# Output slices beside the next image's scan: TensorE adds the two directions in the PSUM bank, VectorE gates from PSUM, ScalarE's copies stand ahead of its decays

## What is computed

```python
xn = layernorm(x) * ln_g + ln_b                       # over the 96 channels
x, z = (xn @ W_in)[..., :192], (xn @ W_in)[..., 192:]
x = silu(causal_conv(x, conv_w, conv_b))              # 4 taps
proj = x @ W_xproj
dt = softplus(proj[..., :6] @ W_dt + b_dt)
h_t = exp(dt_t * A) * h_(t-1) + dt_t * B_t * x_t      # 192 channels x 16 states
y_t = sum over states of h_t * C_t, + x_t * D
out = (y * silu(z)) @ W_out                           # 192 -> 96
```

## Time and profile before

| | |
|---|---|
| time, median of 3 runs (lowest, highest) | 6072.25 us (6064.57, 6073.67) |
| the profiled execution: its own time | 6072.92 us |
| its span in the trace | 6071.1 us |
| VectorE busy, share of the span | 5288.1 us, 87% |
| GpSimd busy | 5088.1 us, 84% |
| TensorE busy (matmuls) | 4711.1 us, 78% |
| ScalarE busy | 3204.5 us, 53% |

### The profile page before, as it was taken

How to read it: one execution, slowest core, us unless ns; L and a number is a source line. 1 busy time by engine, 2 the same in 40 slices (tenths; PEclk the granted TensorE clock), 3 DMA queues, 4 the chain that set the end, 5 groups by cost and what they waited for, 6 DMA issues and landing times. The chain is left out here.

```text
span 6071.1 us, 73617 instructions
## 1 busy us (share of the span) xinstructions
PE 4711.1 (78%) x17230; PEld 1200.4 (20%) x17230; DVE 5288.1 (87%) x3523; ACT 3204.5 (53%) x5159; POOL 5088.1 (84%) x2405
## 2 busy tenths in 40 slices
PE   7998757777777777777777777777777777777788
PEld 6775211111111111111111111111111111111122
DVE  3223749999999999999999999999999999999943
ACT  1224645555555555555555555555555555555533
POOL 0000349999999999999999999999999999999965
PEclk9999876666676666666666666666666666666689
DMA  1002755555555555555555555555555555555599
GB/s 35 28 28 67 213 152 183 184 183 183 184 184 184 184 184 182 182 181 181 182 181 181 182 183 184 184 184 183 182 182 184 184 184 182 183 183 182 182 260 274
DMA packets 351020, 1048.25 MB, mean 173 GB/s; under 512 B 66820, under 2 KB 101430, under 8 KB 300556
## 3 DMA queue, kind: packets, MB, share of 16 engines
q1 hardware_dynamic: 336652, 1022.72, 53.2%
q10 hardware_dynamic: 14336, 25.17, 1.3%
HBM read 836.01 MB, written 211.63 MB: 173 GB/s over the span
## 5 line engine op out<-in xcount | busy, mean ns | idle before, releaser
L1259 POOL TENSOR_TENSOR hc<-hring,c_rep 128x1024 f32<-128x1024 f32 x1541 | 3597.5, 2361 | 18.9 <-DVE hring L1222 13.6
L1222 DVE TENSOR_TENSOR_SCAN hring<-decay,carry,u_ps 128x1024 f32<-128x1024 f32 x1221 | 2827.7, 2333 | 44.3 <-POOL hc L1259 44.3
L1029 PE MATMUL u_ps<-stack_b,w_spread 48*128 48x512 bf16 x2442 | 1053.8, 523 | 908.0 <-DVE hring L1222 904.0
L1116 ACT ACTIVATE decay<-dt_rep,w_a 128x1024 f32<-128x1024 f32 x1222 | 1399.5, 1147 | 675.2 <-DVE hring L1222 662.4
L1204 DVE TENSOR_TENSOR u_ps<-u_ps,u_rep 128x1024 f32<-128x1024 f32 x1221 | 1471.5, 1205 | 68.3 <-DMA u_rep<-u_scr 56.4
L1047 PE MATMUL y_ps<-hc,w_gather 128*32 128x512 f32 x6144 | 1212.4, 874 | 0.0
L1116 ACT ACTIVATE u_ps<-dt_rep,w_a 128x1024 f32<-128x1024 f32 x322 | 360.0, 1118 | 1360.7 <-DVE hring L1222 1360.7
L1246 POOL TENSOR_TENSOR drive_p<-u_rep,b_rep 128x1024 f32<-128x1024 f32 x322 | 760.2, 2361 | 11.1 <-DMA u_rep<-u_scr 11.1
L1222 DVE TENSOR_TENSOR_SCAN hring<-u_ps,carry,drive_p 128x1024 f32<-128x1024 f32 x321 | 751.3, 2341 | 11.6 <-ACT decay L1116 11.6
L666 POOL TENSOR_TENSOR xs<-xc_ln,rs 96x512 f32<-96x512 f32 x64 | 90.3, 1411 | 701.9 <-ACT rs L650 684.2
L1029 PEld LDWEIGHTS u_ps<-stack_b,w_spread 48*128 48x128 bf16 x2442 | 147.4, 101 | 2407.3 <-DVE hring L1222 2004.4
(11 more groups left out here) (108 smaller groups left out, 3966.9 us busy)
## 6 DMA issues: line engine op xcount, KB each, us to landing
dt_rep<-dt_scr SPq DMA_DIRECT2D x194, 1024.0 KB, 5.8
u_rep<-u_scr SPq DMA_DIRECT2D x194, 1024.0 KB, 7.7
c_rep<-bc_scr SPq DMA_DIRECT2D x260, 512.0 KB, 4.0
b_rep<-bc_scr SPq DMA_DIRECT2D x130, 512.0 KB, 4.2
xn<-xn_scr SPq DMA_DIRECT2D x132, 384.0 KB, 5.4
y_scr<-y_sb SPq DMA_DIRECT2D x768, 64.0 KB, 1.6
xn<-xn_scr SPq DMA_DIRECT2D x132, 256.0 KB, 4.7
dt_scr<-dt_sb SPq DMA_DIRECT2D x260, 128.0 KB, 2.1
```

The lines of the kernel that those rows point to most:

```text
L1029: mm = nc.tensor.matmul(u_ps[nv % NSLOT][:, sl], w["spread"][:, q, :], upper(stack_b[drv][:, sl]), start=True, stop=True)
L1116: nc.scalar.activation(to[:, :], dt_rep[r][:, b, :], ACT.Exp, scale=w["a"][:, col:col + 1]).then_inc(decay_ready, 1)
L1222: nc.vector.tensor_tensor_scan(hring[nv % NHR][:, ::step], factor[:, ::step], term[:, ::step], carry[:, drv, nv:nv + 1], ALU.mult, ALU.add ...
L1259: nc.gpsimd.tensor_tensor(hc[nv % NHC][:, :], hring[nv % NHR][:, :], c_rep[q][:, :], ALU.mult).then_inc(c_applied, 1)
```

## The change

In the scan, phases 8 to 63 each also finish one slice of 512 tokens of the image before. `run` has two new tasks. "gate" stands in the phase ahead of a slice: SP loads the slice in step 15 (seven DMAs), TensorE makes z in steps 20 and 22 into `prep_ps`, and ScalarE copies it to `z_sb` a step later each time. "slice" stands in the phase of the slice itself: in steps 0 and 10 TensorE adds the two directions by matmuls with the identity, both into the bank (512 columns, then 256), and VectorE multiplies the bank by `z_sb` into `y_bwd`; Silu of z (768 columns) is done beside that of x in step 0; in step 12 TensorE projects, in step 13 ScalarE copies to `res`, in step 14 SP stores to `out`. Channels stand here as 128 partitions x 512 and, for the last 64 channels, two halves of the tokens on 64 partitions each x 256. The output stage handles only the last image's 8 slices, with the same code in straight line (`over_last`) on buffers of its own. The loop over `it` is cut in three: iterations 0 to 2, 3 written out, 4 to 31. The three j of a conv group now stand together, in steps 14, 16 and 18. ScalarE does in each step what copies out of `prep_ps` first, and its decay last. The weights `z`, `out` and `ident` are prepared in `pointwise`.

```diff
@@ weights, pointwise @@
+            loads.append((self.out_w[rows, col, :], d["w_out"][lo:hi, h, :]))
+        loads.append((w["z"][:, :], d["w_in"][:, DI:2 * DI]))
+        loads.append((w["ident"][:, :], d["ident"]))
...
+                nc.vector.memset(w["out"][:, 1:3, :], 0.0)
...
+                nc.vector.tensor_copy(w["out"][:, 0, :], mixer.out_w[:, 0, :])
+                for s in range(2):
+                    nc.vector.tensor_copy(w["out"][64 * s:64 * s + 64, 1 + s, :], mixer.out_w[64 * s:64 * s + 64, 1, :])
@@ scan: steps @@
-        CONV_AT = ((10, 11, 12), (14, 15, 16), (18, 19, 20))
+        CONV_AT = ((14, 14, 14), (16, 16, 16), (18, 18, 18))
...
+        SLICE_AT, Z_AT = 15, (20, 22)
+        SUM_Y_AT, PROJECT_AT, RES_AT, OUT_STORE_AT = (0, 10), 12, 13, 14
+        CHANNELS = (slice(0, SL), slice(SL, SL + SL // 2))
+        SLICE_DMAS = 7
+        OUT_LAG = 2 * CHUNKS
@@ scan: SP @@
+                def gate(m, k, it, dr):
+                    if m == SLICE_AT:
...
+                        wait(sp, z_made, made, k)
+                        wait(sp, y_sum, summed_y, k)
+                        wait(sp, projected, free, k)
+                        sp.wait_ge(y_stored, stored)
+                        sp.dma_start(xz[:, :], d["xn_scr"][image, :, bass.ds(at + HALO, SL)]).then_inc(slice_in, 16)
+                        for to, scr in ((y_fwd, d["y_scr"][0]), (y_bwd, d["y_scr"][1])):
+                            sp.dma_start(to[:, 0:SL], scr[image, 0:P, bass.ds(at, SL)]).then_inc(slice_in, 16)
+                            for s in range(2):
+                                sp.dma_start(to[64 * s:64 * s + 64, SL:], scr[image, P:DI, bass.ds(at + s * (SL // 2), SL // 2)]).then_inc(slice_in, 16)
@@ scan: TensorE @@
+                            if g == 0 and slicing:
+                                pe.wait_ge(res_ready, pn - 1 - OUT_LAG)
...
+                        if slicing:
+                            pe.wait_ge(gated, 2 * (pn - 1 - OUT_LAG) + 1)
...
+                def gate(m, k, it, dr):
+                    if m == Z_AT[0]:
+                        pe.wait_ge(slice_in, 16 * SLICE_DMAS * (k + 1))
+                        pe.wait_ge(prep_out, NPREP * (k + OUT_LAG + 1) + 3)
+                        nc.tensor.matmul(prep_ps[:, :], w["z"][:, 0:P], xz[:, :], start=True, stop=True).then_inc(z_made, 1)
...
+                def slice_out(m, k, it, dr):
+                    for h in range(2):
+                        if m == SUM_Y_AT[h]:
...
+                            to = prep_ps[:, 0:SL // (h + 1)]
+                            nc.tensor.matmul(to, w["ident"][:, :], y_fwd[:, CHANNELS[h]], start=True, stop=False)
+                            nc.tensor.matmul(to, w["ident"][:, :], y_bwd[:, CHANNELS[h]], start=False, stop=True).then_inc(y_sum, 1)
+                    if m == PROJECT_AT:
+                        pe.wait_ge(gated, 2 * k + 2)
...
-                run(pe, ("front", front), ("back", back), ("prep", prep), ("conv", conv))
+                run(pe, ("front", front), ("back", back), ("prep", prep), ("slice", slice_out), ("conv", conv), ("gate", gate))
@@ scan: ScalarE @@
+                        if slicing:
+                            act.wait_ge(z_out, 2 * (pn - OUT_LAG))
+                            nc.scalar.activation(z_sb[:, :], z_sb[:, :], ACT.Silu).then_inc(z_silu, 1)
...
+                        nc.scalar.copy(z_sb[:, 0:SL], prep_ps[:, :]).then_inc(z_out, 1)
...
+                        nc.scalar.copy(res[:, :], prep_ps[0:C, :]).then_inc(res_ready, 1)
...
-                run(act, ("back", back), ("front", front), ("prep", prep), ("conv", conv))
+                run(act, ("back", back), ("prep", prep), ("slice", slice_out), ("conv", conv), ("gate", gate), ("front", front))
@@ scan: VectorE @@
+                def slice_out(m, k, it, dr):
+                    for h in range(2):
+                        if m == SUM_Y_AT[h]:
+                            dve.wait_ge(y_sum, 2 * k + h + 1)
+                            if h == 0:
+                                dve.wait_ge(z_silu, k + 1)
+                            nc.vector.tensor_tensor(y_bwd[:, CHANNELS[h]], prep_ps[:, 0:SL // (h + 1)], z_sb[:, CHANNELS[h]], ALU.mult).then_inc(gated, 1)
-                run(dve, ("front", front))
+                run(dve, ("front", front), ("slice", slice_out))
@@ output @@
-                over_slices(pe, (2, make_z), (0, project))
+                over_last(pe, (2, make_z), (0, project))
```

More of the change, by code:

```diff
@@ L88, in over_slices, with over_last @@
     image(B - 1, last=True)
+def over_last(eng, *stages):
+    most = max(lead for lead, _ in stages)
+    for s in range(-most, NS):
+        for lead, what in stages:
+            if 0 <= s + lead < NS:
+                what(s + lead)
 def after(eng, sem, count):
@@ L716, in scan @@
         b3 = sb("b3", [P, 3, P])
+        y_fwd = sb("y_fwd", [P, SL + SL // 2])
+        y_bwd = sb("y_bwd", [P, SL + SL // 2])
+        z_sb = sb("z_sb", [P, SL + SL // 2])
+        xz = sb("xz", [C, SL])
+        res = sb("res", [C, SL])
         u_ps = [ctx.enter_context(nc.psum_tensor(f"u_ps{i}", [P, 2 * SL], F32)) for i in range(NSLOT)]
@@ L828, in ahead @@
                         if has == kind:
-                            what(m, pn, 0, pn)
+                            what(m, pn, 0, pn, False)
             ahead("conv", 0)
@@ L837, in run, with iteration @@
             ahead("conv", 1)
-            with eng.Fori(0, ITERS) as it:
+            def iteration(it, gates, slices):
                 for dr in range(2):
@@ L849, in run @@
                             elif kind == "prep":
-                                what(m, p + 1, it + dr, 1 - dr)
-                            else:
-                                what(m, p + 2, it + 1, dr)
+                                what(m, p + 1, it + dr, 1 - dr, slices[dr])
+                            elif kind == "conv":
+                                what(m, p + 2, it + 1, dr, slices[dr])
+                            elif kind == "gate" and gates[dr]:
+                                what(m, p + 1 - OUT_LAG, it + dr, 1 - dr)
+                            elif kind == "slice" and slices[dr]:
+                                what(m, p - OUT_LAG, it, dr)
                     for kind, what in tasks:
@@ L991, in back @@
                                              y_sb[at:at + 32, :]).then_inc(y_stored, 16)
-                run(sp, ("front", front), ("prep", prep), ("conv", conv), ("back", back))
+                def gate(m, k, it, dr):
+                    if m == SLICE_AT:
+                        image, at = slice_of(it)
+                        at = at + dr * SL
+                        made, summed_y, free, stored = ready(2 * k, 2 * k, k, 64 * NG * (k + OUT_LAG - 1))
+                        wait(sp, z_made, made, k)
[8 more added lines that the diff above has]
+                def slice_out(m, k, it, dr):
+                    if m == OUT_STORE_AT:
+                        image, at = slice_of(it)
+                        made, = ready(k + 1)
+                        sp.wait_ge(res_ready, made)
+                        sp.dma_start(d["out"][image, :, bass.ds(at + dr * SL, SL)], res[:, :]).then_inc(out_stored, 16)
+                run(sp, ("front", front), ("prep", prep), ("conv", conv), ("back", back), ("gate", gate), ("slice", slice_out))
                 LAST = 2 * ITERS
                 sp.wait_ge(y_stored, 16 * 4 * NG * LAST)
+                sp.wait_ge(slice_in, 16 * SLICE_DMAS * (LAST - OUT_LAG + 1))
+                sp.wait_ge(out_stored, 16 * (LAST - OUT_LAG))
                 sp.wait_ge(xn_in, 96 * (LAST + 2))
@@ L1382, in _, with multiply @@
-                over_slices(act, (3, gate), (0, store))
+                    act.wait_ge(res_ready, s + 1)
+                    act.dma_start(d["out"][B - 1, :, s * SL:(s + 1) * SL], res[:, r, :]).then_inc(o_stored[r], 16)
+                over_last(act, (3, gate), (0, store))
             @block.vector
             def _(dve):
-                def multiply(b, s):
+                def multiply(s):
                     r = s % R
-                    dve.wait_ge(y_sum, NS * b + s + 1)
-                    dve.wait_ge(z_silu, NS * b + s + 1)
-                    after(dve, projected, NS * b + s - R + 1)
+                    dve.wait_ge(y_sum, s + 1)
+                    dve.wait_ge(z_silu, s + 1)
+                    after(dve, projected, s - R + 1)
```

121 lines of the change are left out of this document (82 added, 39 removed).

## The result

The changed kernel takes 5833.51 us (median of 4 runs, 5826.85 to 5833.89) beside 6071.51 for the kernel before on the same chip: ratio 0.9607, 95% interval 0.9591 to 0.9624, so 238 us faster. The forecast was 5864 us, with 5838 as the lower end. Direction, mechanism and the great term held; the time lies 30 us under the point and 4 us under the range.

What follows compares the result with a forecast made beforehand. GpSimd, late by its one wait a phase for ScalarE's `soft`, was taken to hold VectorE in the scan. 6072.9 - 225 (output stage) - 7 + 3 (VectorE) + 1 (before the scan) + 19 (TensorE) = 5864 us; range 5838 to 5945.

Steps and rivals of the forecast that it cites:

- What bound the scan: Scan: GpSimd's wait for `soft`, 1.14 us a phase, holds VectorE twice, 0.87 us a phase; ScalarE's new order removes it.
- Output stage: Stage after the scan: 8 of 64 slices stay, so it takes about 46.4 us and 225 us go.
- Gates: Scan, 56 phases: two VectorE multiplications, PSUM by SBUF, 0.60 and 0.33 us, together 0.93 us a phase.
- First failed step: VectorE in the scan: unheld it needs 75.52 us a phase, 76.45 with gates; +3 us in 56 phases, -7 in eight.
- Second failed step: TensorE in the scan: one late triple of conv j, 1.3 us, in four phases; +19 us, bounds nothing and 250.
- the sum by it, 5845: Forecast without TensorE's term, on the skill's account that more matmuls make each matmul faster: 5845 us.
- DMA hidden: Scan: slice loads and store, about 1.2 MB a slice, cost nothing, with only 2 to 5 us of cover.
- Before the scan: Pointwise stage: one memset and three small copies, some 0.7 us, entered as +1 us.
- 2: Rival, scan: TensorE late in many phases, costing VectorE 1 to 3.5 us each; 5909 to 6069 us; chance 0.18.
- 4: Rival, scan: TensorE becomes the bound, kernel slower than before; up to 634 us lost, or 6479 us; chance 0.04.
- 3: Rival, scan: GpSimd's wait remains or slice loads land late, gates' 0.93 us on top; 5916 to 5940 us; chance 0.09.
- 5: Rival, more gain: output stage under 40 us and no loss on TensorE; below 5838 us; chance 0.03.

Runs made afterwards that it cites:

- experiment 1: Kernel before, only ScalarE's order changed: copies out of `prep_ps` first in each step, decay last; 5994.58 us, ratio 0.9877.
- experiment 2: Kernel after with ScalarE's old order, decays ahead of what copies out of the bank; 5885.77 us, ratio 0.9696.
- experiment 6: Kernel after, but ScalarE copies each sum from the bank to `y_fwd` and VectorE's gates read SBUF only; 6127.82 us (one run).
- experiment 4: Kernel after with the last j of each conv group one step later; 5826.69 us, ratio 0.9602.
- experiment 3: Kernel before, only the three j of each conv group together, in steps 14, 16 and 18; 6070.1 us (one run).
- experiment 8: Kernel after with the slice loads issued four steps later, step 19 instead of 15; 6177.03 us (one run).

## Why the prediction was right, and where it was wrong

- **What bound the scan** (GpSimd's one wait for `soft` holds VectorE twice; ScalarE's decay to a PSUM slot holds `soft`): shown by experiments 1 and 2, which take the wait away and bring it back alone.
- **Output stage**, 46.4 forecast, 44.4 measured. In the profile it starts at 5787.47, its first z at 5794.93, and the last copy is at 5828.37.
- **Gates**, 0.93 a phase forecast, 76.15 - 75.23 = 0.92 measured. The price held because one operand is in PSUM, as in the row it was taken from; experiment 6 shows what another operand would have made of it.
- **First failed step: "VectorE, if nothing held it, 76.39 - 0.87 = 75.52".** It is 75.23 (experiments 1 and 4, where it waits for nothing). I took off the listed waits, but each of the two costs some 0.08 us more, and a delay of 0.06 that no row lists comes on top; what is left of the 0.29 was not found. So the 56 phases were to be 0.06 longer and are 0.24 shorter: 0.30 x 56 = 17 us, with 1.4 more in the others. That is over half of the miss.
- **Second failed step, a size: "one late triple of 1.3 us in four phases … 19 us".** (1.3 us in one of four phases is 0.325 x 64 = 21; the forecast rounded to 0.3 and got 19.) The mechanism is right (experiment 4 removes it), but it is one triple in six phases, nine times at 0.47 us and once at 1.24: 5.5 us. The 1.3 took a whole triple at 1.2 GHz, and no such one stands in the traces of after or of experiment 3: the longest take 5.5 us instead of 6.0, since the clock rises while a triple runs. The one time that the forecast's price was nearly paid, at 1482.23, the triple was no longer, but the gather ahead of it was slow as well. The mean granted clock rose from 0.67 to 0.74. The Trainium skill (TensorE: Matmul & The Clock Gate, What's actually happening) has it that activity releases the throttle; the traces agree, and the sum by it, 5845, was nearer than my 5864.
- **DMA hidden**: right. I gave the cover as 2 to 5 us; it is about 6, and experiment 8 shows its price.
- **Before the scan**, +1 forecast, +4.3 in the profiled pair: no effect shown. Experiments 6 and 8 have the same code there as the kernel after and reach the first `drive_p` scan at 885.55 and 885.22, against 885.14 before and 889.47 after, so executions differ by that much.
- **The range** was too tight below: its lower end took TensorE's term off but kept VectorE's load as a certainty.

The rest of the 30 us is small: 2 from the output stage, less 3 from what stands ahead of the scan.

The rivals: 2 and 4 (TensorE late, or the bound) fell, as VectorE waits 3.2 us for it in 4271, and 1.1 once before. 3 is what experiment 2 makes, at 5886 us, 30 under its 5916: 17 because 0.31 us a phase of the gates did fall into VectorE's gap, and most of the rest because TensorE's 19 us did not come. 5 is the range in which the time fell, and not for its reasons: the stage took 44.4 us and not under 40, TensorE cost 5.5 us and not nothing, and what made the difference, VectorE's load, is in no rival.

## What to carry to other kernels

Read an engine's own load from start to start in a stretch without waits, not as the period less its listed waits: here that was worth 17 of 30 us. When work moves beside a busy GpSimd, look where VectorE's operands lie: the same multiplication cost 0.67 us with one of them in PSUM and 5.5 with both in SBUF. And a load that is hidden has a place in the queue on which this depends; the same loads four steps later made the kernel slower than before the change. Take the length of a step from the phase (here 76.15 / 24), not from one instruction.

## What the runs showed of the hardware that I had not expected

- VectorE's multiplication with two SBUF operands stood through two of GpSimd's instructions in a row (5.50 us in the mean for 512 columns, 0.85 for 256), while GpSimd kept its 2.38 us.
- A long group of matmuls that began at 1.2 GHz lifted the clock during its own run: 5.38 and 5.49 us for six passes, and 0.62 instead of 1.03 us for the spread right behind.
- A wait costs its listed idle time and 0.08 to 0.09 us more, the overlap of one VectorE instruction with the next.
